# Masking the four-head attention units on VectorE, between the taps of a later convolution

## The reference, cut to what matters

```
x2 = (x[..., :, None] * x[..., None, :]).reshape(b, h, l, f * f) / R2
ones = jnp.ones((b, h, l, 1), dtype=x.dtype)
return jnp.concatenate([ones, x / RRD, x2 / RD], axis=-1)
...
kv = k[..., None, :] * v[..., :, None]
kv = jnp.cumsum(kv, axis=2)
num = jnp.einsum('bhlD,bhldD->bhld', q, kv)
den = jnp.einsum('bhlD,bhlD->bhl', q, jnp.cumsum(k, axis=2)) + EPS
y = num / den[..., None]
```

## Time and profile before

| | us |
|---|---|
| median of 3 timed runs | 531.67 (530.93 to 533.12) |
| the profiled execution | 526.27 |
| its span, first to last instruction | 524.5 |
| TensorE busy | 419.3 (80%) |
| VectorE busy | 283.7 (54%) |
| ScalarE busy | 139.9 (27%) |
| GpSimd busy | 101.5 (19%) |
| granted TensorE clock, mean share of full speed | 0.905 |

### The profile page before, as it was taken

The page is one execution under the profiler, slowest core; times in us unless marked ns, Lnnn a source line. Parts: engine busy times, 40 slices in busy tenths (PEclk is TensorE's granted clock), DMA queues, the critical chain, the costliest instruction groups (busy, mean ns, idle before and its releaser), DMA issues.

```text
span 524.5 us, 7875 instructions
## 1 busy us (share of the span) xinstructions
PE 419.3 (80%) x2734; PEld 307.0 (59%) x2739; DVE 283.7 (54%) x810; ACT 139.9 (27%) x184; POOL 101.5 (19%) x126
## 2 busy tenths in 40 slices
PE   3868989797988889988979987108999999992086
PEld 1257647423855346733667276006999999992065
DVE  5885942693885969672440014771344444341943
ACT  0100130384304842067332930102212212220000
POOL 1000000243001600024000410274223322331500
PEclk9978998899999999999996997557999999997559
DMA  7198059600794018800299472133011111102303
GB/s 238 43 311 189 1 121 134 136 2 8 143 142 101 1 34 152 146 2 1 80 155 277 181 183 90 44 128 64 24 45 45 33 43 45 45 17 46 98 1 121
DMA packets 27073, 48.14 MB, mean 92 GB/s; under 512 B 9621, under 2 KB 23477, under 8 KB 25253
## 3 DMA queue, kind: packets, MB, share of 16 engines
q1 hardware_dynamic: 25174, 43.92, 36.7%
q0 software_dynamic: 1872, 3.86, 2.0%
HBM read 37.58 MB, written 12.45 MB: 95 GB/s over the span
## 4 chain that ended last, share of the span: by engine, by line
PE 51%; DVE 21%; DMA 8%; ACT 6%; issue 5%; POOL 5%; SPq 3%; DVEq 0%; ACTq 0%; POOLq 0%
PE ring L1278 12%; PE att L1288 9%; DVE wide L678 7%; PE ring L1073 5%; PE att L1171 4%; PE ring L1161 4%; DMA w1b<-k_parts 4%; ACT probs L558 3%; POOL tokens_by_expert L507 3%; PE ring L1092 3%; PE att L1038 2%; POOL probs L498 2%; PE misc L1203 2%; PE ring L1053 1%; DMA w<-in_x 1%
## 5 line engine op out<-in xcount | busy, mean ns | idle before, releaser
L498 POOL TENSOR_SCALAR_AFFINE_SELECT probs<-probs 128x256 f32<-128x256 f32 (+1 forms) x72 | 40.5, 568 | 260.8 <-ACT probs L558 260.7
L558 ACT ACTIVATE probs<-ring,ones 128x1024 f32<-128x1024 f32 (+2 forms) x72 | 65.2, 971 | 26.4 <-PE ring L1161 25.9
L678 DVE SCALAR_TENSOR_TENSOR wide<-w,wdw,wide 96x512 f32<-96x512 f32 x90 | 65.6, 795 | 0.2
L1038 PE MATMUL att<-idle 128*128 128x256 bf16 x282 | 40.7, 313 | 24.9 <-DMA tokens_by_expert<-x_all,pos_i 22.7
L1038 PEld LDWEIGHTS att<-idle 128*128 128x128 bf16 x282 | 31.4, 113 | 32.9 <-issue 23.2
L1288 PE MATMUL att<-w,probs 128*128 x276 | 48.7, 326 | 0.8 <-DVE probs L903 0.8
L520 POOL DMA_INDIRECT ffn_by_token<-probs,target x23 | 32.2, 1399 | 86.1 <-DVE probs L910 86.1
L1288 PEld LDWEIGHTS att<-w,probs 128*128 128x128 f32 x276 | 44.3, 190 | 1.1 <-issue 1.1
L1161 PE MATMUL ring<-w1b 128*128 128x384 bf16 (+3 forms) x188 | 37.0, 312 | 9.5 <-ACT probs L558 5.8
L1171 PE MATMUL att<-probs,va 128*32 128x512 f32 (+3 forms) x384 | 37.9, 454 | 5.1 <-POOL probs L498 4.2
L635 ACT ACTIVATE probs<-ring 128x768 f32<-128x768 f32 x23 | 18.7, 811 | 84.2 <-PE ring L1278 84.2
(11 more groups left out here) (220 smaller groups left out, 576.1 us busy)
## 6 DMA issues: line engine op xcount, KB each, us to landing
w1b<-q_parts SPq DMA_DIRECT2D x32, 192.0 KB, 7.7
w1b<-k_parts SPq DMA_DIRECT2D x8, 576.0 KB, 15.4
w<-in_w SPq DMA_DIRECT2D x1, 4608.0 KB, 28.3
w<-in_x SPq DMA_DIRECT2D x4, 768.0 KB, 11.6
w1a<-in_w1a SPq DMA_DIRECT2D x1, 2304.0 KB, 13.5
q_parts<-q_area SPq DMA_DIRECT2D x24, 96.0 KB, 2.1
k_parts<-k_area SPq DMA_DIRECT2D x24, 96.0 KB, 2.1
w1b<-in_w1b SPq DMA_DIRECT2D x1, 2304.0 KB
```

The source lines that it names most:

```text
L498: nc.gpsimd.affine_select(diag, diag, [[0, len(UNITS[n][1])], [1, P]], ALU.is_ge, minus_one, base=0, channel_multiplier=-1).then_inc(p_rea ...
L558: nc.scalar.activation(squares(n), bank[:, :, 0:N - P * j], ACT.Square, bias=ones[:, 0:1], scale=0.25).then_inc(sq_done, 1)
L678: ins = nc.vector.scalar_tensor_tensor(dst, src, w, dst, ALU.mult, ALU.add)
L1038: nc.tensor.matmul(bank[:, 0:2 * P], idle[:, 0:P], idle[:], start=True, stop=True)
```

## The change

For units 12 to 17, the mask moves from GpSimd to VectorE. Instead of a selection it is a minimum with a table `limit`, which is a huge number on and below the diagonal of (key, query) that is kept and -1 elsewhere; a square is never below 0. GpSimd keeps the pairs. The values of quads wait for a semaphore of their own, p4_ready. In attend(0) and attend(1) VectorE also computes the first half of the convolution of batch b + 2, which stood at the end of front(b + 1): taps 0 and 1 behind the mask of unit 12, and one tap behind the mask of each of units 13 to 17. In attend(2) and attend(3) there are masks alone. The table is one more DMA (64 KB) at the end of ATTN, into a buffer that is otherwise unused until after the attention.

```diff
+        limit = incl[:].rearrange("p e t -> p (e t)")
...
-        p_ready = sem("weights_ready")
+        p_ready, p4_ready = sem("weights_of_pairs_ready"), sem("weights_of_quads_ready")
...
-                (wo, "wo"), (pick, "pick"), (sel, "sel"), (pref, "pref"), (steps, "steps"), (ones, "ones")]
+                (wo, "wo"), (pick, "pick"), (sel, "sel"), (pref, "pref"), (steps, "steps"), (ones, "ones"), (limit, "limit")]
...
             def attend(b):
-                for n in range(NU):
+                for n in range(FIRST_QUAD):
                     pool.wait_ge(sq_done, NU * b + n + 1)
...
-            def convolve(b, halves=(0, 1)):
+            def convolve(b, halves=(0, 1), steps=range(TAPS)):
...
-                    for tap in range(TAPS):
+                    for tap in steps:
...
+                    if TAPS - 1 not in steps:
+                        continue
                     st.settle()
...
                 if b == 0:
                     convolve(1, (1,))
-                elif b < B - 1:
-                    convolve(b + 1, (0,))
...
             def attend(b):
-                pass
+                for n in range(FIRST_QUAD, NU):
+                    dve.wait_ge(sq_done, NU * b + n + 1)
+                    diag = squares(n)[:, :, 0:P]
+                    nc.vector.tensor_tensor(diag, diag, limit[:, None, :].to_broadcast([P, len(UNITS[n][1]), P]),
+                                            ALU.min).then_inc(p4_ready, 1)
+                    at = n - FIRST_QUAD
+                    if b + 2 < B:
+                        convolve(b + 2, (0,), range(at + (at > 0), at + 2))
...
-                    pe.wait_ge(p_ready, NU * b + n + 1)
+                    if n < FIRST_QUAD:
+                        pe.wait_ge(p_ready, FIRST_QUAD * b + n + 1)
+                    else:
+                        pe.wait_ge(p4_ready, (NU - FIRST_QUAD) * b + n - FIRST_QUAD + 1)
...
+    o["limit"] = np.where(p[None, :] >= p[:, None], np.finfo(f).max, -1.0).astype(f)
```

## The result

The changed kernel runs in 543.55 us (median of 4, 542.45 to 545.1), the kernel before in 532.39 (median of 4, 530.93 to 533.54); the ratio is 1.0305, 95% interval 1.0255 to 1.0354. The kernel before varies between executions from 524 to 539 us; the ratios in this document compare fast executions alone, and this one stands for some 527.5 us of the kernel before (543.55 / 1.0305), which is why it lies above the quotient of the two medians, 1.021. The prediction was 544.6 (539.5 to 550.0). The profiled execution has a span of 541.8 us, 17.3 more than that of before.

The account below looks back on a forecast made before the run. It took the chain through the quads' GpSimd masks into project's transposes as the bound. Table 0.5, VectorE order 10.4, batches 2 and 3 0.2 and clock 1.8 gave 12.9 us; on 531.67, 544.6 us (539.5 to 550).

Parts of the forecast that it names:

- The order on VectorE: Quads of batches 0 and 1: masks queue behind taps in VectorE's list, losing 4.9 and 5.5 us, +10.4 us.
- a minimum takes 690 ns: One quad mask on VectorE, 128 x 512 floats, estimated from nearby rows at 690 ns, bounds 557 and 1020.
- The spacing and not the duration counts: VectorE instructions overlap: a tap instruction costs 0.66 us, a minimum 0.62, so rounds of 1.95; 2.17 without overlap.
- The table: One more DMA behind `ones` delays ScalarE's first copy and all behind it: +0.47 us, bounds 0 and 0.9.
- Batches 2 and 3: Quads with masks alone, 690 against 634 ns, two in series with squares: +0.1 us for each batch, +0.2 together.
- A sign that did not hold: Expected in the later profile: GpSimd's mask line L498 with 48 instructions in place of 72, none over some 0.5 us.
- The clock: TensorE, mostly waiting in late quads, drops to half rate for project(1) or project(2): one fall, +1.8 us, bounds 0 and 3.6.
- The base: The 12.9 us sum, made on the profiled 526.27 us, was added to the runs' median of 531.67, 5.4 us above.
- The rival with two falls: The clock falls in both batches, 546.4 us, or the minimum is near 1020 ns, to 551; chance 0.25.
- Not slower: Rival: taps and masks in the quads fit the squares' pace, the run wins 1.7 us, 530.0; chance 0.04.
- its own decision point: Round length in the quads at which taps and masks would fit the old 5.83 us: 0.57 us a round.

Follow-up runs that it names:

- e2: The change with all seven taps behind the mask of unit 17 in attend(0) and attend(1): 527.4 us, ratio 1.0011 to the kernel before.
- e6: The change with one convolution instruction (half a tap) between two masks, the other nine behind the mask of unit 17: 535.1 us, ratio 1.0148.
- e9: e6 plus idle TensorE products, five before the waits of units 15 to 17, eight behind the transposes of project(1) and project(2): 527.8 us, ratio 1.0000.
- e3: The kernel before with only the taps moved as in the change; all masks on GpSimd, no table: 528.3 us, ratio 1.0019.
- e7: The change with taps 0 to 3 ahead of batch 0's attention masks, tap 0 ahead of batch 1's, the rest behind unit 17's mask: 526.2 us, ratio 0.9986.
- e8: The tap order of e7, but with all masks on GpSimd as in the kernel before and no table: 526.3 us, ratio 0.9967.
- e5: The kernel before with only the quads' masks moved to VectorE; the half convolution stays whole ahead of the attention's masks: 539.5 us, ratio 1.0243.
- e10: The kernel before plus idle TensorE products, four before the waits of units 16 and 17, eight behind the transposes of project(1) and project(2): 528.3 us, ratio 0.9994.
- e11: e8 plus the same idle TensorE products as e10: 527.0 us, ratio 0.9995.
- e1: The kernel before, run again unchanged, ten executions: 526.3 us, ratio 1.0003.

## Why the prediction was right, and where two errors cancelled

- **The order on VectorE: right, in place and size.** Forecast: first gap 2.87, rounds of 1.95, last mask's end at 11.36, +10.4 us in both batches. Measured: 2.84, 1.93, 11.22, and +4.9 and +5.6. That a minimum takes 690 ns was right (672 to 695 over 24). Taps behind (e2) and half taps (e6) scale it as the sum has it.
- **The spacing and not the duration counts.** 0.66 us for a tap's instruction and 0.60 for a minimum of 0.69. The rule in the Trainium skill, "VectorE: DVE Perf Modes", section "The DRAIN you can't avoid", taken without its exception would have given rounds of 2.17; the trace has 1.93.
- **The table: wrong, +0.47 forecast, -0.08 measured.** The issue is one slot later, but the loads land together:

```profile
28.62 0.43 SPq L368 DMA_DIRECT2D ones<-in_ones  x1
29.09 0.43 SPq L368 DMA_DIRECT2D incl<-in_limit  x1
...
33.50 0.87 ACT L540 ACTIVATE gh<-ring 128x384 f32<-128x384 f32 x2 [13.56 <-DMA incl<-in_limit]
```

  The lower bound, 0, was the case; ScalarE's release is no later than in the earlier trace rows.
- **Batches 2 and 3:** +0.2 forecast, under 0.1 measured, hidden behind ScalarE.
- **A sign that did not hold:** GpSimd has the 48 masks of pairs that were forecast, but one of them took 840 ns where none was to be over some 500; the median is 407.
- **The clock: the mechanism right, the size too low.** This is the step that failed. I had one fall at 1.8 us, and 3.6 as the upper bound; both batches fell, and it was 2.9 and 3.3 us in the projects alone, 6.2 together. I priced a fall from the pairs of batch 0, where ScalarE and the masks cover part of a slow TensorE. Here it hits L1100, where TensorE alone is on the path, and 3.69 us become 5.71, or 7.07 in e6. The price of a low clock has to be read from the stage that it falls in. The Trainium skill, "TensorE: Matmul & The Clock Gate", section "Part 1: The HAM clock gate (the "warmup" mystery)", has the rule that too little activity halves the rate; by it both projects would start slow, and the trace agrees (0.50 from 124.1 to 134.4, and 0.50 from 198 to 204).
- **The base.** The sum was made on one profile and moved to a median 5.4 us above it. The sum gave 12.9 us where the spans of the profiles differ by 17.3 (and 16.1 by the ratio, 543.55 - 527.5); on the medians the difference is 11.2. So 544.6 came near 543.55 by luck: a clock term that was 4.4 us too low met a base that was too high by about as much. That the 5.4 were themselves clock, which longer executions of the kernel before lose, is likely by the clocks of the executions below, but no trace of such an execution shows it.

The rival with two falls had the mechanism best, though its 3.6 us were too few as well. "Not slower" fell with its own decision point: a round of 0.57 us was needed, and it was 1.93.

What stays open: no long execution of the kernel before was profiled, so that the clock falls in its project(1) or project(2) is argued from the runs below and not seen. The one long execution that was profiled, e9's, lost its time elsewhere.

## What to carry to other kernels

Work that fills an engine's gaps is only free if nothing that others wait for stands behind it in the same in-order list; a filler between two urgent steps must be shorter than the slack of each step, not than the sum. Before moving a step off a contended engine, ask whether the contention or the order costs: here e3, e7 and e8 differ by some 2 us, while the order, with the clock that it took along, was worth 16. And when a change makes TensorE wait, count the wait, and then ask in which stage a low clock would fall and how much work TensorE gets before the next one: in the change, short work between waits carried the low clock into project (3 us a batch); in e5 the waits were longer, but dense work stood behind them, and project started at full clock. These are two cases and no rule.

## What the runs showed of the hardware

- GpSimd's selection and VectorE's two-input taps slow each other to a common pace. Alone they take 634 and 738 ns, together five masks took 5.0 us (e3). Moving the masks to VectorE or the taps out of the way ends this; both gave quads of 5.6 us.
- The clock seems to sit at an edge in this kernel. The longest of the 24 executions of e10 and e11, with idle products, took 532.4 us. Of the 34 executions of e2, e7 and e8, whose quads are 5.6 us, none took over 530.5. Of the 86 executions of the kernel before (76 beside the experiments and e1's ten), 27 took over 532.4. Among the 28 beside e9 to e11 the mean granted clock goes with the time: 0.903 to 0.910 at 524.6 to 527.3 us, 0.891 to 0.897 at 532.8 to 536.1, 0.882 to 0.885 at 538.8 to 539.5. This fits a fall behind the masks that some 1 us more or less of them decides, at 8 or 14 us, but it is not shown: the idle products of e10 and e11 also stand in project, and in e9's long execution the clock fell between the pointwise products and the next attention, 1.2 to 1.6 us for each of two batches by the distances, with the quads at full clock.
- In e6 masks that ended 6.6 us after the first had begun, little later than in batch 0 before (6.5), were followed by a low clock in project's first eight products (0.50 from 124.8 to 131.6); the medians 535.1 and 527.8 (e9) are the price.
